# T2's lower part is fetched from memory for each couple of tiles, and Strassen's form takes 832 of the 1,024 columns in place of 712

## The reference, cut to what matters

```python
x = x + _L0_cond_ref(...)   # x W0^T + 2 * (top-2 of 8 gated experts of rank 16)
x = x + _L1_cond_ref(...)   # per batch element: a 64x64 matrix mixes the 64 rows
x = x + _L2_cond_ref(...)   # adapter of rank 16, picked by an id
x = x + _L3_cond_ref(...)   # x W3^T + b + 2 * (adapter of rank 16, picked by an id)
```

## Time and profile before

| | us |
|---|---|
| median of 3 runs | 901.65 |
| lowest, highest | 899.28, 902.4 |
| profiled execution, its own time | 900.0 |
| its span, first to last instruction | 898.2 |
| TensorE busy | 890.5 (99%) |
| VectorE, ScalarE, GpSimd busy | 585.0, 346.4, 243.7 |

### The profile page before, as it was taken

One profiled execution on the slowest core, in us unless ns is written; L12 is line 12 of the kernel. 1 busy time (PEld: TensorE's weight loads), 2 busy tenths in 40 slices (PEclk: granted clock), 3 DMA queues, 4 the chain that ended last, 5 costly groups with the idle time before them and its releaser, 6 DMA issues.

```text
span 898.2 us, 14951 instructions
## 1 busy us (share of the span) xinstructions
PE 890.5 (99%) x4726; PEld 791.1 (88%) x4726; DVE 585.0 (65%) x1575; ACT 346.4 (39%) x800; POOL 243.7 (27%) x379
## 2 busy tenths in 40 slices
PE   8999999999999999999999999999999999999997
PEld 7888888888888888998998998998998999999997
DVE  6555444444357536777777767777767778777776
ACT  5543343333234323434434434424434334334333
POOL 2010010011110004523524515415415325235240
PEclk9999999999999999999999999999999999999999
DMA  6988686999663564666756756757657667657664
GB/s 240 308 261 294 210 248 201 306 335 283 198 187 109 167 207 147 182 189 188 227 176 188 240 159 193 230 163 212 206 166 228 185 179 220 193 174 220 191 200 150
DMA packets 105604, 187.71 MB, mean 209 GB/s; under 512 B 15926, under 2 KB 66870, under 8 KB 105526
## 3 DMA queue, kind: packets, MB, share of 16 engines
q1 hardware_dynamic: 105526, 186.76, 68.0%
HBM read 143.20 MB, written 49.81 MB: 215 GB/s over the span
## 4 chain that ended last, share of the span: by engine, by line
PE 95%; DMA 2%; DVE 1%; SPq 1%; issue 0%; ACT 0%; DVEq 0%
PE ps_o L1405 28%; PE ps_d L1431 19%; PE ps_w L1439 13%; PE ps_d L1439 10%; PE ps_s L1405 9%; PE ps_o L1452 5%; PE ps_d L1446 4%; PE ps_o L1463 3%; PE ps_s L1469 1%; DMA mdraw<-t 1%; PE ps_w L1446 1%; DMA stat_raw<-stat 1%; PE ps_s L1484 1%; PE ps_o L1496 0%; SPq L446 0%
## 5 line engine op out<-in xcount | busy, mean ns | idle before, releaser
L1041 DVE TENSOR_TENSOR stat_lo<-stat_raw,stat_hi 128x1024 fp32r<-128x1024 f32 (+1 forms) x127 | 142.3, 1121 | 46.1 <-ACT stat_hi L772 43.8
L772 ACT ACTIVATE stat_hi<-stat_raw 128x1024 fp32r<-128x1024 f32 (+1 forms) x127 | 116.8, 933 | 17.3 <-POOL stat_raw L656 4.9
L1431 PE MATMUL ps_d<-w_hi,stat_hi 128*128 128x512 f32 x256 | 103.4, 404 | 0.0
L1431 PE MATMUL ps_d<-w_lo,stat_hi 128*128 128x512 f32 x256 | 101.1, 395 | 0.0
L1431 PE MATMUL ps_d<-w_hi,stat_lo 128*128 128x512 f32 x256 | 100.8, 394 | 0.0
L1405 PE MATMUL ps_o<-chunk_a_hi,stat_hi 128*128 128x512 f32 x216 | 84.4, 391 | 1.1 <-DVE stat_lo L1041 1.1
L1405 PE MATMUL ps_o<-chunk_a_hi,stat_lo 128*128 128x512 f32 x216 | 84.1, 389 | 0.0
L1405 PE MATMUL ps_o<-chunk_a_lo,stat_hi 128*128 128x512 f32 x216 | 84.1, 389 | 0.0
L656 POOL TENSOR_TENSOR stat_raw<-stat_raw,ident 128x128 f32<-128x128 f32 x40 | 23.6, 590 | 183.6 <-DMA stat_raw<-stat 183.6
L681 POOL CAST w_hi<-mdraw 128x512 fp32r<-128x512 f32 x32 | 25.1, 784 | 160.1 <-DMA mdraw<-t 153.5
L1405 PE MATMUL ps_o<-chunk_b_hi,stat_hi 128*128 128x512 f32 x152 | 59.1, 389 | 0.0
(11 more groups left out here) (223 smaller groups left out, 2287.8 us busy)
## 6 DMA issues: line engine op xcount, KB each, us to landing
up<-tu SPq DMA_DIRECT2D x124, 256.0 KB, 4.5
stat_raw<-stat SPq DMA_DIRECT2D x59, 512.0 KB, 4.5
mdraw<-t SPq DMA_DIRECT2D x128, 208.0 KB, 3.1
stat_raw<-x SPq DMA_DIRECT2D x32, 512.0 KB, 3.5
out<-outb SPq DMA_DIRECT2D x30, 512.0 KB, 5.1
t<-md_a SPq DMA_DIRECT2D x16, 576.0 KB, 6.0
rows_raw<-x SPq DMA_DIRECT2D x32, 256.0 KB, 3.9
chunk_a_raw<-mov SPq DMA_DIRECT2D x24, 256.0 KB, 5.2
```

The costliest lines, as they stand in the source:

```text
L772: return nc.scalar.activation(dst, src, ACT.Copy)
L1041: return nc.vector.tensor_tensor(out=dst, in0=src, in1=rounded.bitcast(F32), op=ALU.subtract)
L1431: last = nc.tensor.matmul(plain_bank(t)[:, 0:WCOLS], rows[a][:, k, :], w[c][:, k, :], start=k == 0 and m == 0, stop=k == KB - 1 and m == l ...
```

## The change

T2's lower part no longer has a place of its own. In setup it is made in the place of `mdraw` (`T2_made`), SP stores it to memory (`t2_lower`) at `M_DONE + 3`, and `choose(0)` and `load_md(0)` move from `M_DONE` to `M_DONE + 4`, behind a wait for that store. In every step SP loads it (`load_t2(j)`, 852 KB at the new width) into the place of x_a (raw and part of hi), after P2 has read x_a for the last time; P6 takes the two passes with T2's upper part over all four blocks first, then waits for the load and takes the third (`streamed`). `load_x0(j+1)` now waits for P6. SP's, ScalarE's and VectorE's orders in a step change with it. SH goes from 356 to 416: WCOLS from 512 to 392, PL from 312 to 192, the pieces from 376, 356, 356 to 256, 416, 416 columns.

```diff
-STRASSEN = 356
+STRASSEN = 416
...
+    t2_lower = nc.dram_tensor("t2_lower", (P, HALF_KB, SH), F32R, kind="Internal").ap()
...
-        T2raw, T2 = split_pair("T2", HALF_W)
+        T2_hi = sb("T2_hi", HALF_W, F32R)
...
+            if at(n, X0_AT):
+
+                with nc.sbuf_tensor("T2_lo", HALF_W, F32R) as T2_lo:
+                    pass
             raw, both = split_pair(f"stat{n}", [P, KB, P])
...
+        assert HALF_KB * SH <= 2 * BT * FULL
+        with ExitStack() as first:
+            T2raw = first.enter_context(nc.sbuf_tensor("T2_raw", HALF_W, F32))
+        with ExitStack() as first:
+            T2made = first.enter_context(nc.sbuf_tensor("T2_made", HALF_W, F32R))
+        T2 = [T2_hi, T2_lo]
         mdraw = sb("mdraw", [P, 2 * BT, FULL], F32R)
...
             def load_x0(j):
...
-                    sp.wait_ge(pe_p[1], j)
+                    sp.wait_ge(pe_p[5], j)
...
+            def load_t2(j):
+                sp.wait_ge(pe_p[1], j + 1)
+                if at(j, 0):
+                    sp.wait_ge(st_t2, 16)
+                sp.dma_start(T2_lo[:, :, :].bitcast(F32), t2_lower.bitcast(F32)).then_inc(ld_t2, 16)
...
                 if g == M_DONE:
...
+                if g == M_DONE + 3:
+                    sp.wait_ge(dve_t, HALF_KB)
+                    sp.dma_start(t2_lower.bitcast(F32), T2made[:, :, :].bitcast(F32)).then_inc(st_t2, 16)
+                if g == M_DONE + 4:
                     choose(0)
+                    sp.wait_ge(st_t2, 16)
                     load_md(0)
...
             def step(j, back, fin):
...
-                load_x0(j + 1)
+                load_t2(j)
                 if back:
                     load_up2(b1)
+                choose(a + 2)
                 choose(b + 2)
                 if back:
                     load_up3(b1)
+                load_x0(j + 1)
+                load_md(a + 2)
                 load_s2(j + 1)
-                choose(a + 2)
-                load_md(a + 2)
                 load_s3(j + 1)
...
@@ ScalarE, step
                 fore(j, back, fin)
-                x0_hi(j + 1)
                 hgT_hi(a)
...
                     h2_hi(b1)
+                x0_hi(j + 1)
                 ud_hi(a + 2)
...
@@ VectorE, fore and step
                 s_lo(j, 3)
+                if back:
+                    hidden_rows(b1)
...
                 fore(j, back, fin)
-                x0_lo(j + 1)
                 hgT_lo(a)
...
                 hidden_rows(a)
+                x0_lo(j + 1)
                 plain_lo(b)
                 Rb_lo(j)
-                hidden_rows(b)
                 mix_lo(a)
...
@@ TensorE
+            def streamed(ps, rows, weights, arrived, count):
+
+                for passes in (PASSES[:2], PASSES[2:]):
+                    for k in range(HALF_KB):
+                        for a, c in passes:
+                            last = nc.tensor.matmul(ps[:, 0:SH], rows[a][:, k, :], weights[c][:, k, :], start=False,
+                                                    stop=k == HALF_KB - 1 and at(c, lo), skip_group_check=True)
+                    if at(len(passes), 2):
+                        pe.wait_ge(arrived, count)
+                return last
...
-                winograd(ps_w, S[1], T2, False).then_inc(pe_p[5], 1)
+                streamed(ps_w, S[1], T2, ld_t2, 16 * (j + 1)).then_inc(pe_p[5], 1)
...
-                experts(a, plain_bank(a)[:, HL:HALF], YP).then_inc(pe_xp, 1)
+                experts(a, plain_bank(a)[:, HL:WCOLS], YP).then_inc(pe_xp, 1)
```

More of the change, by code:

```diff
@@ L178, in build @@
         kept_bytes = 2 * (KB * WCOLS + 3 * HALF_KB * SH) * 4
-        gap_bytes = 8 * HALF_KB * SH * 4 - 2 * KB * HALF * 4
+        gap_bytes = 7 * HALF_KB * SH * 4 - 2 * KB * HALF * 4
         assert 0 <= gap_bytes and 2 * PER * 2 * ROW * 4 <= kept_bytes + gap_bytes
@@ L222, in build @@
         up2 = up2_wide[:, BR:BR + D]
-        hole_a = sb("hole_a", [P, 2 * KB * HALF])
-        assert late_bytes <= 2 * KB * HALF * 4
+        hole_a = sb("hole_a", [P, max(2 * KB * HALF, late_bytes // 4)])
         sraw, st = [], []
@@ L331, in build @@
         ld_up2_b, ld_up3_b = sem("ld_up2_b"), sem("ld_up3_b")
+        ld_t2, st_t2 = sem("ld_t2"), sem("st_t2")
         st_own, st_out, st_last = sem("st_own"), sem("st_out"), sem("st_last")
@@ L606, in last @@
                 load_mix(b1, b1)
+                load_t2(j)
                 load_up2(b1)
                 load_mix(b, TURN_B)
-                sp.wait_ge(pe_p[1], PAIRS)
+                load_up3(b1)
+                sp.wait_ge(pe_p[5], PAIRS)
                 up_rows(chosen2.pop(b), tu2, up2_b, ld_up2_b)
-                load_up3(b1)
                 store_out(a1)
@@ L822, in t_hi @@
                 act.wait_ge(dve_t4, n + 1)
-                for raw, both in ((T1raw, T1), (T2raw, T2), (T3raw, T3), (T4raw, T4)):
+                for raw, both in ((T1raw, T1), (T2raw, (T2_hi, T2made)), (T3raw, T3), (T4raw, T4)):
                     last = round_to(both[hi][:, n, :], raw[:, n, :])
@@ L919, in plain_hi @@
                 act.wait_ge(pe_xp, t + 1)
-                round_to(y[t % 2][hi][:, YP], plain_bank(t)[:, HL:HALF]).then_inc(act_yp, 1)
+                round_to(y[t % 2][hi][:, YP], plain_bank(t)[:, HL:WCOLS]).then_inc(act_yp, 1)
             x0_hi(0)
@@ L1251, in plain_lo @@
                 dve.wait_ge(act_yp, t + 1)
-                rest(y[t % 2][lo][:, YP], plain_bank(t)[:, HL:HALF], y[t % 2][hi][:, YP]).then_inc(dve_yp, 1)
+                rest(y[t % 2][lo][:, YP], plain_bank(t)[:, HL:WCOLS], y[t % 2][hi][:, YP]).then_inc(dve_yp, 1)
             def bias_piece(turn, n, dst):
@@ L1597, in step @@
                 pe.wait_ge(pool_mb, b + 1)
-                experts(b, plain_bank(b)[:, HL:HALF], YP).then_inc(pe_xp, 1)
+                experts(b, plain_bank(b)[:, HL:WCOLS], YP).then_inc(pe_xp, 1)
                 pe.wait_ge(dve_La_raw, j + 1)
```

## The result

The changed kernel takes 902.96 us, the median of 7 runs (901.32 to 904.72). The kernel before, timed beside it in 7 runs, takes 899.28 (898.49 to 902.40). The ratio is 1.0032, with a 95% interval of 1.0018 to 1.0047: slower by 0.3%, where 0.6% faster was predicted. The profiled execution of the changed kernel took 901.32 us with a span of 899.5; that of before took 900.0 with a span of 898.2. So there are 1.3 us to explain in the two traces, and 6.8 against the forecast of -5.5. The granted clock, as a mean over the span, is 1.000 after and 0.999 before, so it is no part of the difference.

A forecast was written before the change was run, and what follows sets the result against it. TensorE was taken as the bound, busy 890.5 of 898.2 us. Widths -4.0 and waits -1.5 made -5.5 us: 894.5 against the profiled 900.0, 896.1 against the median; range 890.5 to 902.5.

The forecast's parts named there:

- Setup: Some ten VectorE instructions in each of four setup blocks, about 60 ns longer each, with 1.55 us idle there: cost 0.
- The rest: Closing terms: setup 0, later rows of tile 0 0, and a wait of 0.2 to 0.3 us in the last step.
- Rival C: Pace of the couples' new widths differs: 1% slower gives 901.6 us, 1% faster 890.6; 10% each.
- Widths: Matmuls of the steps at their new column counts: each step 0.27 us shorter, 4.0 us for 15 steps.
- 110 ns: Price of any matmul with a 128-column load, so the 192-column piece of `ranks3` takes 110 ns, not 89.
- T2's load: 852 KB on SP's queue in each of 16 couples, landing in 4.3 us before P6's third pass needs it: cost 0.
- cover: Spare time of T2's lower-part load before P6 must wait: 2.7 us; past it every us late costs a us.
- the 7.0 us: Latest time after P2 at which T2's lower part may land without making P6 wait.
- Rival A: T2's lower part lands late: P6 waits 0.7 us in 16 couples, 11.2 us, time 907; 10%.
- x_a later, VectorE's slack: x_a is loaded only after P6: cost 0, with VectorE's slack 1.2 us before `plain_lo(b)` and 0.4 at `mixed(a1)`.
- Five of six waits gone: `h3_rows` loses five of six waits for VectorE as `hidden_rows(b)` leaves its place before `h3_lo`: 1.5 us saved.
- `last` +0.2 to 0.3: In `last`, `hgT_lo(a)` comes late for `experts(a)`: a wait of 0.2 to 0.3 us, eating that step's 0.27.

The follow-up runs named there:

- e1_chunk384: The changed kernel with setup's moving chunks 384 bytes further on in each partition; 895.81 us, ratio 0.9958 to the kernel before.
- e3_before_both128: The kernel before with setup's chunks and stationary tiles both 128 bytes further on; 897.78 us, ratio 0.9989.
- f5_load_later: e1_chunk384 with the load of T2's lower part one place later on SP, behind the second adapter rows of b1; 926.47 us.
- f3_hidden_first: The kernel before with only hidden_rows(b1) moved on VectorE, into the next couple's first part where x0_lo stood; median 899.42 us, ratio 0.9996.

## Why the prediction was wrong, point by point

- **Setup: wrong, and this is the miss.** The step that failed is in "The rest": "Setup: ... 0". It priced the wider VectorE instructions and asked what they delay, but took the pace of setup's matmuls for given. They went from 226.7 to 232.4 ns, 5.7 ns on each of 1,464, 8.3 us by the rows; the couples began 7.8 us later (TensorE's waits for data in setup were 0.9 us, where they were 1.1 before; the other 0.3 us I haven't traced). `e1_chunk384` gives it all back with one number in a size.
- **Rival C had the cause in its hand.** It said that "the pace depends on something besides the width" and "may come out differently with new row lengths and places", from 227 against 233 ns at the same 512 columns. `e3_before_both128` shows what that something was in part: for the first couple's `plain(a)` 233 became 226.7, in the later couples only 229.5 in the mean. But the rival was priced on the couples alone, 5.5 us for 1%. There the pace held, near enough. The 1,464 matmuls of setup, whose addresses the change moves as well, were left out. With them in, its slow half would have been 896.1 + 5.5 + 3.3 (1% of 333 us) = 904.9, and the range would have reached there.
- **Widths: right.** Forecast 0.27 us a step; 34.41 became 34.07 to 34.18, in the mean 0.30 less. Twelve matmuls of 392 columns took 2.13 to 2.15 us (2.15 forecast), of 416 columns 2.26 to 2.29, in P7 2.35 (2.27 forecast). The slope held although the distances changed. A likely reason is that rows of 1664 and 1424 bytes begin at ever new distances; the kernel with TensorE alone has them within 2% wherever they begin. For the rows of 392 columns this was not tried. The piece of `ranks3` with 192 columns did not take 110 ns: its start-to-start interval was 88, but the wider piece behind it took 208 to 216 where others of its width take 189, so the pair took as long as the 110 would have made it.
- **T2's load: right at 0 in the profile**, 4.7 us against 4.3, cover 2.3 against 2.7, and `f5_load_later` bears the 7.0 us out. The 4.0 us that the prediction worked out as an estimate come from a formula that the Trainium skill, page DMA: Bandwidth & Descriptors, section Anatomy of one DMA, fits to transfers on GpSimd's path; this one goes out on SP's queue and took 4.7. Rival A put the danger in all couples at once; it is real in one of 16, about 0.8 us, so some 0.8 us a run in the mean is missing from the sum.
- **x_a later, VectorE's slack: right.** No wait in front of `plain(a)` beyond the couples' beginning, none at `mixed`.
- **Five of six waits gone, 1.5 us: right in the sum**, for all six went, 1.7 us. The reason given, the place of `hidden_rows`, is not borne out: with it alone four of six waits stay (`f3_hidden_first`), and without it five of six went in `e3_before_both128`.
- **`last` +0.2 to 0.3: near**, 0.4 us of wait.

The couples as a whole: -5.5 forecast, -6.5 in the profile. Put together with a setup at its old pace (`e1_chunk384`), the ratio is 0.9958, -3.8 us; the forecast 896.1 against 895.81 is luck in part, since that run carries 2 us of waits that I had at 0 and the kernel before ran 2 us faster than the median that I started from.

## What to carry to other kernels

When a change alters the size of anything in a hand-packed memory, list the addresses of the operands of **every** hot loop before and after, also of loops that the diff doesn't touch, and count their matmuls as a term of the sum. Where the profile shows one instruction form at two paces (227 and 233 ns here), that is a measured effect with an unknown cause: price it on all instructions of that form, both ways, or settle it first by comparing the operands' addresses at the two places. With moving rows of 2048 bytes, a distance of 0 modulo 256 bytes to the stationary tile was worth 2.5% of TensorE's time in setup, for a few hundred bytes of padding; in the steps of the couples it was worth 0.3% (34.41 to 34.32 us). So measure each loop; don't carry the 2.5% over.

## What the runs showed of the hardware

- A stream of fp32r matmuls of 512 columns, each with a load of 128 columns, takes 226.7 ns a matmul where the moving rows stand at 0 modulo 256 bytes from the stationary tile, 228.3 at 16, 228.9 at 64, 231.9 at 48, and 232.4 to 234.3 at 32, 96, 128, 160, 192, 224 and 240. It needs no traffic of other engines, and comes out the same within 0.3 ns in the setup of a full kernel and in a kernel with nothing but these matmuls (16.32 and 16.34 us for 72, 16.73 and 16.73, 16.48 and 16.49). In the couples of a full kernel, at distance 0, such matmuls took 229.5 ns in the mean. I had not expected such an effect at all, and still have no mechanism for it.
- Distances that alternate between 0 and 128 cost as much as a steady 128 (233.3 ns).
- At 416 and 356 columns the effect is about 2% and has another order: 186.7 ns at 192, 188.3 at 0 for 416. Even the best blocks (226.7, 186.7 and 160.0 ns) stand above columns over 2.4 GHz: 213.3, 173.3 and 148.3 ns. The page TensorE: Matmul & The Clock Gate of the Trainium skill, section Back-to-back issue gap, gives that quotient plus 2.5 ns for the isolated gap of one matmul; these streams, with a load for each matmul, come down to it at no distance tried.
- A transfer of 832 KB that lands in 4.2 to 4.9 us in most couples took 7.5 to 8.0 in 6 of 96, with nothing different in the program.
- In `f5_load_later` TensorE's granted clock fell to 1.2 GHz for 3.4 us three times, behind or at the end of waits of 1.9, 1.9 and 3.1 us, and matmuls of 416 columns took 346 ns there. Its 12 other waits for the load, one of 3.1 us among them, had no such sequel.
